# Third expert's weights asked for one gather earlier, and one tile fewer turned by TensorE

## The reference, cut to what matters

```
x = hidden_states.reshape(-1, H)                 # 2048 tokens, H = 512
topk_w, topk_idx = top_k(softmax(x @ gate_w.T), 2)
g = einsum('th,eih->tei', x, w_gate)             # 16 experts, INTER = 352
u = einsum('th,eih->tei', x, w_up)
h = silu(g) * u
expert_out = einsum('tei,ehi->teh', h, w_down)
y = einsum('te,teh->th', combine, expert_out)    # then x + y
```

## Time and profile before

| what | us |
|---|---|
| median of three runs | 348.83 (348.81 to 350.17) |
| profiled execution | 347.8 |
| its span | 346.0 |

### The profile page before, as it was taken

How to read it: one execution, slowest core, us unless ns; L and a number is a source line. 1 busy time by engine, 2 the same in 40 slices (tenths; PEclk the granted TensorE clock), 3 DMA queues, 4 the chain that set the end, 5 groups by cost and what they waited for, 6 DMA issues and landing times.

```text
span 346.0 us, 7810 instructions
## 1 busy us (share of the span) xinstructions
PE 335.8 (97%) x1879; PEld 297.1 (86%) x1879; DVE 233.8 (68%) x307; ACT 179.0 (52%) x242; POOL 129.7 (37%) x85
## 2 busy tenths in 40 slices
PE   8999999999999899999999999999999999999992
PEld 4777878789899799899999999999999998989981
DVE  0586799988453558484878857788667588779320
ACT  1498711622546373655567554675545575575321
POOL 0000000023344461566284653757535271444323
PEclk9999999999999999999999999999999999999997
DMA  7991963847479899998999997899988969921153
GB/s 288 388 488 53 426 245 119 294 152 251 160 224 307 242 210 325 228 294 230 306 297 265 340 324 197 240 293 322 298 212 235 264 195 279 317 36 29 14 76 44
DMA packets 47352, 82.22 MB, mean 238 GB/s; under 512 B 5488, under 2 KB 22000, under 8 KB 47216
## 3 DMA queue, kind: packets, MB, share of 16 engines
q1 hardware_dynamic: 38336, 62.70, 54.9%
q0 software_dynamic: 8960, 18.89, 25.0%
HBM read 60.59 MB, written 19.92 MB: 233 GB/s over the span
## 4 chain that ended last, share of the span: by engine, by line
PE 91%; DMA 3%; DVE 2%; issue 1%; ACT 1%; POOLq 1%; DVEq 0%; ACTq 0%; POOL 0%
PE bank L693 43%; PE bank L722 23%; PE bank L449 4%; PE bank L667 4%; PE bank L549 4%; PE bank L553 4%; PE bank L550 4%; DMA xg<-y_rows,gidx 2%; PE bank L465 1%; PE bank L480 1%; PE bank L625 1%; PE bank L576 1%; DMA y_rows<-y_st 1%; POOLq L96 0%; DVE hh L1165 0%
## 5 line engine op out<-in xcount | busy, mean ns | idle before, releaser
L1250 POOL DMA_INDIRECT out<-ys,sidx x40 | 76.4, 1911 | 118.2 <-DMA out<-ys,sidx 71.0
L1229 POOL DMA_INDIRECT xg<-y_rows,gidx x40 | 52.7, 1319 | 94.4 <-issue 79.4
L693 PE MATMUL bank<-w_hi,xt_hi 128*128 x320 | 82.0, 333 | 0.3 <-issue 0.3
L355 DVE TENSOR_TENSOR w_lo<-w_raw,w_hi (+2 forms) x32 | 76.2, 2382 | 8.8 <-issue 5.9
L693 PE MATMUL bank<-w_hi,xt_lo 128*128 x320 | 79.0, 323 | 0.0
L693 PE MATMUL bank<-w_lo,xt_hi 128*128 x320 | 79.0, 323 | 0.0
L353 ACT ACTIVATE w_hi<-w_raw (+2 forms) x32 | 64.7, 2021 | 8.6 <-DMA w_raw<-wall 4.6
L847 ACT ACTIVATE sg<-bank 128x352 f32<-128x352 f32 x40 | 18.5, 462 | 75.6 <-PE bank L693 75.6
L693 PEld LDWEIGHTS bank<-w_lo,xt_hi 128*128 128x128 f32 x320 | 56.2, 189 | 0.0
L693 PEld LDWEIGHTS bank<-w_hi,xt_lo 128*128 128x128 f32 x320 | 56.1, 189 | 0.0
L693 PEld LDWEIGHTS bank<-w_hi,xt_hi 128*128 128x128 f32 x320 | 54.6, 189 | 1.4 <-issue 0.7
(11 more groups left out here) (181 smaller groups left out, 364.0 us busy)
## 6 DMA issues: line engine op xcount, KB each, us to landing
w_raw<-wall SPq DMA_DIRECT2D x16, 1408.0 KB, 8.0
w_raw<-wall SPq DMA_DIRECT2D x16, 768.0 KB, 9.8
xs<-xg SPq DMA_DIRECT2D x128, 64.0 KB
x_st<-xin SPq DMA_DIRECT2D x8, 512.0 KB, 13.3
y_rows<-y_st SPq DMA_DIRECT2D x16, 256.0 KB, 4.1
head_sb<-head SPq DMA_DIRECT2D x2, 640.0 KB, 5.1
wb_sb<-wb SPq DMA_DIRECT2D x2, 512.0 KB, 8.9
wbt_sb<-wbt SPq DMA_DIRECT2D x2, 512.0 KB, 10.8
```

The lines of the kernel that those rows point to most:

```text
L355: e.tensor_tensor(w_lo[:, bass.ds(dst, n)], raw, hi, ALU.subtract).then_inc(own, 1)
L693: mm = e.matmul(bank[2 + 2 * s + t % 2][:, 0:INTER], a, w[:, bass.ds(at + (k * GU + s * INTER), INTER)], start=k == 0 and i == 0, stop=k = ...
L1229: e.indirect_dma_start(out=xg[t % NXG][:], out_offset=None, in_=y_dram, in_offset=bass.IndirectOffsetOnAxis(ap=gidx[:, t:t + 1], axis=0)). ...
L1250: e.indirect_dma_start(out=out, out_offset=bass.IndirectOffsetOnAxis(ap=sidx[:, t:t + 1], axis=0), in_=ys[t % NYS][:], in_offset=None, bou ...
```

## The change

The number of the gather behind which SyncE starts the later weights goes from 4 to 3, that is from the fifth to the fourth gather. `N_PE` goes from 8 to 7, so tile 7 is copied by SyncE and turned by VectorE in place of TensorE. The number of `later_weights` calls ahead of the first `rows_apart` was `N_PE - N_COPY + 1` = 4 and is now the constant `N_SOON` = 4. SyncE's list thus stays the same, but for `rows_apart(7)` which comes in between `later_weights(3)` and `rows_apart(8)`.

```
-N_PE, NXS = 8, 4
-N_LEAD, N_COPY = 9, 5
+N_PE, NXS = 7, 4
+N_LEAD, N_COPY, N_SOON = 9, 5, 4
...
-C_SECOND, N_LATE = CH - 1, 4
+C_SECOND, N_LATE = CH - 1, 3
...
             e.wait_ge(d_g[N_LATE], 16)
-            for t in range(N_PE - N_COPY + 1):
+            for t in range(N_SOON):
                 later_weights(t)
             for t in range(N_PE, NTILE + N_COPY):
                 if t < NTILE:
                     rows_apart(t)
-                if N_PE < t < NTILE - NRAW + N_COPY:
+                if N_SOON <= t - N_COPY < NTILE - NRAW:
                     later_weights(t - N_COPY)
```

## The result

The changed kernel takes 346.75 us (median of 8 runs, 346.17 to 347.49), against 349.56 for the kernel before on the same chip (8 runs, 348.81 to 352.39). The ratio is 0.9932, with a 95% interval of 0.9907 to 0.9957. It is a gain of some 0.5%, 1.7 us. Single runs that fell into a slower state of the chip are left out of all medians and ratios here.

The account below looks back on a forecast made before the run. The prediction took TensorE, busy 97% of the span, as the bound. Terms of -1.5, -0.46 and +0.5 summed to -1.46 us, carried over to a median of 347.4 us, with a range of 346.4 to 349.5.

Parts of the forecast that it names:

- The bound and the old wait: TensorE busy 97% of the span; h_turn(4) 1.87 us late, traced to the landing of the third expert's gu.
- The term of the ask: Third expert's weights asked for 3.5 us earlier, ScalarE's gu split starts near 104.5: -1.5 us, between 0 and -1.87.
- The rest of a wait that I left: At h_turn(4): foretold to start at 112.9, against the 112.54 given by the pace.
- The term of the transposes: TensorE's x_turn(7) of 0.48 us goes; by the pace, 6.76 against 6.30, worth -0.46 us.
- The copy's landing: Tile 7's copy, awaited by VectorE ahead of its transposition in round 4, lands at 114.8, 0.3 us late.
- bound (a): Tile 7's copy is asked for after gather 7 lands at 106.8 and takes 8.1 us: 114.9.
- bound (b): Tile 7's copy queues behind the fourth expert's dn, landing at 113.7: copy at 114.7, or 117.7 at worst.
- The term of the new wait: VectorE's wait for tile 7's copy delays h_low(4) and TensorE: +0.5 us, bounds 0 and 3.2.
- The deadline: down(4) due at 117.8, 4.9 us behind h_turn(4); tile 7's transposition must start by 114.5.
- What I expected for tile 8: Its copy, landing no earlier than before, delays down(5), due at 124.1: 1.0 us in all, half of it taken.
- Rival 1: Copies of tiles 7 and 8 land in time, nothing given back: -1.96, at most -2.33, 346.9 to 346.5; chance 0.24.
- Rival 3: Tile 7's copy caught behind the fourth weights, VectorE's in-order list delays TensorE: slower, 350.1 at 117.7; chance 0.10.

Follow-up runs that it names:

- e1: Changed kernel plus two bounding masks, but TensorE still turns tile 7, so only the weights' ask is moved: 347.33 us, ratio to before 0.9946.
- e3: Changed kernel plus two masks, with VectorE's transposition of tile 7 moved one round later, behind h_low(4) and y_low(6): 345.89 us, ratio to before 0.9917.
- e6: Kernel with the earlier ask plus two masks, TensorE turning tiles 0 to 8, first copy tile 9's: 347.69 us, ratio to before 0.9967.
- c1: Changed kernel plus only two masks that bound loaded numbers: ratio to before 0.9951.
- c3: Changed kernel plus the two masks, measured again on another occasion: 347.63 us, ratio to before 0.9964.
- e5: Changed kernel plus two masks, with the weights asked for one more gather earlier, behind the third: ratio to before 0.9948.
- e2: Changed kernel plus two masks, but weights asked for behind the fifth gather again, so only tile 7 is moved: 351.54 us, ratio to before 1.0067.
- e7: The kernel with tile 7's transposition moved one round later, measured again beside the changed kernel on one chip: 346.77 us, ratio to before 0.9934.

## Why the prediction was right, step by step

**The bound and the old wait.** Right. With the ask 3.5 us earlier the round of 8.63 fell to 6.81.

**The term of the ask, -1.5: too small in size.** It measured -1.82 (8.63 to 6.81). The step that was off is the gap between silu and the split. I took 0.42 us from another round; in the changed kernel it was 0.24. I had also rounded 104.38 up to 104.5. The split started at 104.21 on before's clock. The rest of a wait that I left, 0.36, was 0.05. That nothing else came late (gather 4) is right: `x_turn(4)` waited for nothing.

**The term of the transposes, -0.46.** Right: 0.48 between e1 and e3, 0.57 between e1 and e6.

**The copy's landing, 114.8.** Right in place, and near exact in this execution: 115.25 less 0.47 is 114.8. That agreement is luck. Two errors in bound (a) cancel: gather 7 took 7.3 us and not 8.3, so the copy was begun at 105.8 and not 106.8, and then it took 9.0 us and not 8.1. In bound (b) the fourth `dn` landed at 111.9 and not 113.7, and the copy came 2.8 us behind it and not 1.0. On before's clock the other executions of this order have it at 115.0 (c1), 114.4 (c3) and, with the still earlier ask, 115.8 (e5).

**The term of the new wait, +0.5: too small.** `down(4)` lay 5.64 us behind `h_turn(4)`, where 4.67 is free of waits: 0.97 us, and in the others 0.56 (c3) and 1.24 (c1). This is the term that was mis-sized most. The deadline was 117.3 and not 117.8: 0.3 of that is the old wait, gone more fully than I had it, and the rest that I took 4.9 us from `h_turn(4)` to `down(4)`, where 4.67 is free of waits. I also left out the 0.25 us between the end of `h_low(4)` (118.46) and the first matmul of `down(4)` (118.71), which e2 and c1 show too. The same copy was that much more late. What I expected for tile 8 did not come: its copy landed earlier as well, and `down(5)` waited for nothing. The ring rule of the Trainium skill (DMA: Bandwidth & Descriptors, section Queues, rings and completion order), by which the descriptors of one queue are taken in order on each DMA engine, fits e5, where the copy came 0.8 us behind the `dn`; in the changed kernel it came 2.8 behind. Which of the two bounds held the copy is open, as said under e5.

**The sum.** -1.82 - 0.46 + 0.97 = -1.31, and the stretch itself shrank by 1.28 (38.68 to 37.40). That this is near the -1.46 of the forecast is in part because its two errors, -0.3 and +0.5, have opposite signs. The profiled execution was 1.2 us faster: 1.28 in the stretch, less the 0.47 by which it began later, and 0.39 behind the stretch that the change does not explain. The median fell by 2.8 us, or 2.4 by the ratio; over all three measurements of the change it is 1.3 to 2.4. The forecast of 347.4 lies 0.65 above the measured 346.75, inside the range. I gave "within 0.5%" the most, 0.63. The three ratios lie on both sides of that line, and the first, at 0.68%, beyond it.

**The rivals.** Rival 1 did not come in the change, but e3 is it, made by hand: both terms and nothing given back. Rival 3's mechanism, VectorE's in-order list behind the copy, is what e2 shows: the transposition started at 119.1 and 3.3 us were given back (8.02 against 4.75). The old wait stood there as well, so the deadline was later than in the rival, and its price list does not carry over as it is. The earlier ask kept the change from it.

**What stays open.** The first measurement of the change gave more than its profile does, by some 1.2 us. Single times of all these kernels scatter by 1 to 2 us. Three sources are shown. One is the wait ahead of `h_turn(4)` in the kernel before. One lies ahead of all that was changed: over the thirteen profiled executions `x_turn(2)` starts between 89.58 and 90.72. The third stands in e7's profiled execution, in ScalarE's timeline near tile 17:

```profile
186.67 2.56 ACT L353 ACTIVATE w_hi<-w_raw  x1 [2.81 <-DMA w_raw<-wall]
189.14 0.44 ACT L847 ACTIVATE sg<-bank 128x352 f32<-128x352 f32 x1
```

There ScalarE waited 2.81 us for a later expert's `gu`, silu behind it waited, and TensorE lost 1.3 us; in the changed kernel's execution the same idle time was 0.79 us, which costs nothing. How much of the scatter, and of the difference between profile and median, the three make was not measured.

## What to carry to other kernels

A wait in a full pipeline is worth what it holds up down to the next deadline, so moving its cause gave its full 1.8 us. Work moved to an engine with time to spare has to be placed in that engine's list: ahead of the result that the critical engine awaits, one wait on a late transfer cost more than the work saved, and the same instruction three entries later cost nothing. Two edits made together should be run alone as well: here one carried the whole gain, and the other lost 2.4 us, gave back what it won, or won 0.5 us according to its company.

## What the runs showed of the hardware that I had not expected

- A copy of 256 KB within the on-chip memory, in four transfers of 64 KB, was waited for until 8.1 to 10.1 us after its first issue (before 8.1, changed kernel 9.0, c1 9.1, e2 10.0, e5 10.1), with weights and gathers on the way. In e1 tile 8's was there after at most 5.9 us.
- The same 768 KB transfer of the third `dn` took 11.3, 10.2 and 12.4 us as it was asked for at 97.0, 94.0 and 93.3. It landed at 108.3, 104.2 and 105.7, each on its own execution's clock and in one execution each: the earliest ask did not give the earliest landing.
